# Cross-attention: the group maxima of the keys are copied between partition groups by ACT instead of being turned by TensorE

## The reference

```python
a = _layer_norm(audio_kv, ln_gamma, ln_beta)
Q = (hidden_states @ Wq.T) ...      # (B, 16, 512, 64)
K = (a @ Wk.T) ...
V = (a @ Wv.T) ...
scores = einsum('bhtd,bhsd->bhts', Q, K) * scale, masked keys at -inf
attn = softmax(scores, axis=-1)
out = einsum('bhts,bhsd->bhtd', attn, V) ... @ Wo.T
return hidden_states + tanh(gate) * out
```

## Time and profile before

| | |
|---|---|
| median of three runs | 2112.95 us |
| profiled execution, its own time | 2124.67 us |
| its span | 2122.9 us |
| granted clock of TensorE, mean | 0.992 |
| PE busy | 2024.5 us, 95% |
| DVE busy | 1709.6 us, 81% |
| POOL busy | 1510.0 us, 71% |
| ACT busy | 1127.6 us, 53% |
| share of PE in the chain that ended last | 71% |
| share of DVE in it | 18% |

### The profile page before, as it was taken

The page is one execution under the profiler, slowest core; times in us unless marked ns, Lnnn a source line. Parts: engine busy times, 40 slices in busy tenths (PEclk is TensorE's granted clock), DMA queues, the critical chain, the costliest instruction groups (busy, mean ns, idle before and its releaser), DMA issues.

```text
span 2122.9 us, 25985 instructions
## 1 busy us (share of the span) xinstructions
PE 2024.5 (95%) x8960; PEld 1589.0 (75%) x8960; DVE 1709.6 (81%) x2236; ACT 1127.6 (53%) x1578; POOL 1510.0 (71%) x830
## 2 busy tenths in 40 slices
PE   6999999999999999999999999999989999999996
PEld 4777777777777777777777777777767777777774
DVE  7788678887888878888788887888788888788785
ACT  4665744546544565445654556454554545644542
POOL 5999986567766687567866588666866668765664
PEclk9999999999999999999999999999999999999998
DMA  6566535444355334545236443355333553344331
GB/s 250 211 235 223 192 129 191 176 164 144 126 189 194 132 129 160 177 166 179 102 141 228 152 141 141 125 216 189 113 124 128 210 190 115 136 160 154 129 119 62
DMA packets 137219, 342.00 MB, mean 161 GB/s; under 512 B 56576, under 2 KB 57600, under 8 KB 136192
## 3 DMA queue, kind: packets, MB, share of 16 engines
q1 hardware_dynamic: 137088, 340.33, 45.5%
HBM read 288.89 MB, written 51.38 MB: 160 GB/s over the span
## 4 chain that ended last, share of the span: by engine, by line
PE 71%; DVE 18%; POOL 4%; issue 3%; ACT 3%; DMA 1%; SPq 1%; POOLq 0%; ACTq 0%; DVEq 0%
PE pj L435 13%; PE pj L439 13%; PE pj L437 12%; PE sc L387 5%; DVE prob L732 5%; PE sc L354 5%; PE sc L355 5%; PE sc L391 4%; PE sc L388 4%; PE pv L379 3%; PE pv L380 3%; DVE m_b L726 3%; DVE xy L777 2%; DVE mq L707 2%; PE pv L365 1%
## 5 line engine op out<-in xcount | busy, mean ns | idle before, releaser
L933 POOL TENSOR_TENSOR p_lo<-prob,p_hi 128x1024 fp32r<-128x1024 f32 x256 | 615.8, 2416 | 199.6 <-ACT p_hi L551 199.6
L707 DVE TRANSPOSE_TENSOR_REDUCE mq<-sc 128x32 f32<-128x1024 f32 x256 | 304.7, 1227 | 160.9 <-PE sc L355 160.7
L439 PE MATMUL pj<-a_hi,w_lo 128*128 128x512 f32 x1024 | 407.0, 397 | 0.0
L437 PE MATMUL pj<-a_lo,w_hi 128*128 128x512 f32 x1024 | 405.9, 396 | 0.0
L435 PE MATMUL pj<-a_hi,w_hi 128*128 128x512 f32 x1024 | 400.8, 391 | 3.6 <-POOL a_lo L967 1.4
L777 DVE SCALAR_TENSOR_TENSOR xy<-sc,tg_b,xy 128x1024 f32<-128x1024 f32 x256 | 321.1, 1272 | 42.9 <-PE sc L391 36.6
L570 ACT COPY o_tmp<-pv 64x512 f32<-64x512 f32 x128 | 74.3, 581 | 524.7 <-PE pv L380 524.6
L937 POOL TENSOR_TENSOR prob<-prob 128x1024 f32<-128x1024 f32 x128 | 308.2, 2408 | 0.0
L732 DVE TENSOR_TENSOR prob<-sc,m_b 128x1024 f32<-128x1024 f32 x256 | 301.5, 1219 | 4.4
L944 POOL TENSOR_TENSOR r_b<-o,r_b 128x512 f32<-128x512 f32 x64 | 83.3, 1302 | 311.5 <-DVE r_b L749 311.5
L546 ACT ACTIVATE prob<-prob 128x1024 f32<-128x1024 f32 x256 | 271.6, 1061 | 9.2 <-DVE prob L732 4.6
(11 more groups left out here) (88 smaller groups left out, 3854.2 us busy)
## 6 DMA issues: line engine op xcount, KB each, us to landing
w_hi<-kept_hi SPq DMA_DIRECT2D x225, 512.0 KB, 3.7
w_lo<-kept_lo SPq DMA_DIRECT2D x225, 512.0 KB, 4.6
cx<-in_ctx SPq DMA_DIRECT2D x32, 512.0 KB, 7.1
xy<-in_xT SPq DMA_DIRECT2D x32, 512.0 KB, 6.5
kept_hi<-w_hi SPq DMA_DIRECT2D x32, 512.0 KB, 5.6
kept_lo<-w_lo SPq DMA_DIRECT2D x32, 512.0 KB, 6.3
out_y<-xy SPq DMA_DIRECT2D x7, 2048.0 KB, 9.8
w_raw<-in_wq SPq DMA_DIRECT2D x8, 512.0 KB, 5.2
```

Source lines behind the costliest of these rows:

```text
L437: pe.matmul(dst[:, 0], w_hi[:, w, cols], s_lo[:, i], start=False, stop=False)
L439: mm = pe.matmul(dst[:, 0], w_lo[:, w, cols], s_hi[:, i], start=False, stop=i == KT - 1)
L707: dve.tensor_reduce(out=mq[:, 2 * i:2 * i + 2], in_=sc[:, 2 * i:2 * i + 2].rearrange("p s (b j) -> p s b j", j=32), op=ALU.max, axis=mybir ...
L933: pool.tensor_tensor(p_lo[:, 2 * i:2 * i + 2], prob[:, h, 2 * i:2 * i + 2], f32(p_hi[:, 2 * i:2 * i + 2]), ALU.subtract).then_inc(pl_done, 1)
```

## The change

The two PE transposes of a half go, with one DVE reduction and the tiles `m_cols`, `m_rows` and `m_two`. In their place ACT copies the 32x16 pieces of `m_own` (the new name of the 128x16 maxima) from the four partition groups side by side into partitions 0 to 31 of `m_four` (`gather_maxima`, four copies), DVE reduces them into the first group of `m_all` (`key_maxima`, 32x16), and ACT copies that group to the three others (`hand_out_maxima`, three copies). `spread_maxima` reads `m_all` in SBUF where it read a bank of `pv`. Each of the seven copies is an instruction of its own.

The names of two DVE functions change place: `group_maxima` is now the 128x16 reduction and `key_maxima` the one that combines the groups.

`FILL` is now (5, 4, 5, 2, 20) for half 0 and (5, 4, 7, 2, 18) for half 1: with the transposes gone there is one piece less, and the first number that follows the second `values` is 5 or 7, where it was 2 behind a 5 and a 2.

On ACT the new copies stand, in half 0, behind `o_high` (and behind the first `x_high` of "prepare", and the four `a_high` of "switch") and ahead of `split_w`, the other three `x_high` and `o_move`; in half 1 behind the second `q_high` and ahead of `split_w`, four `x_high` and `o_move`.

```diff
-FILL = ((5, 5, 2, 2, 2, 20), (5, 5, 2, 2, 2, 20))
+FILL = ((5, 4, 5, 2, 20), (5, 4, 7, 2, 18))
...
-            def maxima_turned(k, h):
-                pe.wait_ge(mc_done, k * 2 + h + 1)
-                ge(pe, oadd_done, k * 2 + h - 1)
-                pe.transpose(pv[h][:, 0, 0:P], m_cols[:], ident[:]).then_inc(mf_done, 1)
-
-            def maxima_back(k, h):
-                pe.wait_ge(mr_done, k * 2 + h + 1)
-                pe.transpose(pv[h][:, 0, P:2 * P], m_rows[:].rearrange("p c i -> p (c i)"), ident[:]).then_inc(mt_done, 1)
...
+            def gather_maxima(k, h):
+                act.wait_ge(mo_done, k * 2 + h + 1)
+                for c in range(4):
+                    act.copy(m_four[:, c], m_own[groups[c]]).then_inc(mf_done, 1)
+
+            def hand_out_maxima(k, h):
+                act.wait_ge(ma_done, k * 2 + h + 1)
+                for g in range(1, 4):
+                    act.copy(m_all[groups[g]], m_all[groups[0]]).then_inc(mv_done, 1)
...
-                split_w(b, WV, j + 1)
                 if kind == "prepare":
-                    for i in range(KT // 2):
-                        x_high(k, b, i, (b + 1) % 2)
+                    x_high(k, b, 0, (b + 1) % 2)
                 if kind == "switch":
                     for i in range(KT // 2, KT):
                         a_high(k, b, i)
+                gather_maxima(k, 0)
+                hand_out_maxima(k, 0)
+                split_w(b, WV, j + 1)
+                if kind == "prepare":
+                    for i in range(1, KT // 2):
+                        x_high(k, b, i, (b + 1) % 2)
                 if begun:
                     o_move(k - 1, 1)
...
                     q_high(k, 1)
+                gather_maxima(k, 1)
+                hand_out_maxima(k, 1)
+                if not last:
                     split_w(b, WQ, j + 2)
...
             def key_maxima(k, h):
+                dve.wait_ge(mf_done, k * 8 + 4 * h + 4)
+                dve.tensor_reduce(out=m_all[groups[0]], in_=m_four[:].rearrange("p c b -> p b c"), op=ALU.max,
+                                  axis=mybir.AxisListType.X).then_inc(ma_done, 1)
...
             def spread_maxima(k, h):
-                dve.wait_ge(mt_done, k * 2 + h + 1)
+                dve.wait_ge(mv_done, k * 6 + 3 * h + 3)
                 dve.transpose(m_b[:].rearrange("p (b i) -> p b i", i=32),
-                              pv[h][:, 0, P:P + 16].rearrange("p (b o) -> p b o", o=1).to_broadcast((P, 16, 32))
-                              ).then_inc(mb_done, 1)
+                              m_all[:].rearrange("p (b o) -> p b o", o=1).to_broadcast((P, 16, 32))).then_inc(mb_done, 1)
```

More of the change, by code:

```diff
@@ L72, in xattn_kernel @@
         m_b, r_b = sb("m_b", [P, T]), sb("r_b", [P, T])
-        mq, m_cols, m_rows = sb("mq", [P, TB, 16]), sb("m_cols", [P, P]), sb("m_rows", [P, 4, 32])
-        m_two = sb("m_two", [P, 64])
+        mq, m_own = sb("mq", [P, TB, 16]), sb("m_own", [P, 16])
+        m_four, m_all = sb("m_four", [32, 4, 16]), sb("m_all", [P, 16])
         rq, r_four = sb("rq", [P, 2, 16]), sb("r_four", [P, 4, 16])
@@ L103, in xattn_kernel @@
         init_done, row_done, mask_done, mrow_done = sem("init_done"), sem("row_done"), sem("mask_done"), sem("mrow_done")
-        mq_done, mc_done, mg_done, mr_done, mb_done, sub_done = (
-            sem("mq_done"), sem("mc_done"), sem("mg_done"), sem("mr_done"), sem("mb_done"), sem("sub_done"))
+        mq_done, mo_done, mf_done, ma_done, mv_done, mb_done, sub_done = (
+            sem("mq_done"), sem("mo_done"), sem("mf_done"), sem("ma_done"), sem("mv_done"), sem("mb_done"), sem("sub_done"))
         rq_done, rsum_done, rinv_done, rb_done = sem("rq_done"), sem("rsum_done"), sem("rinv_done"), sem("rb_done")
@@ L138, in xattn_kernel @@
         halves = (slice(0, HD), slice(HD, P))
+        groups = [slice(32 * g, 32 * (g + 1)) for g in range(4)]
         def splits(b, kind, pair):
@@ L373, in values @@
             def values(k, h, i):
-                if i == 0 and h == 0:
-                    pe.wait_ge(vl_done, k + 1)
+                if i == 0:
+                    ge(pe, oadd_done, k * 2 + h - 1)
+                    if h == 0:
+                        pe.wait_ge(vl_done, k + 1)
                 pe.wait_ge(pl_done, k * 4 + 2 * h + i + 1)
@@ L470, in body @@
                         pe.wait_ge(mrow_done, 2)
-                        pe.wait_ge(init_done, 7)
+                        pe.wait_ge(init_done, 5)
                     if j == 0 and h == 0 and not (isinstance(k, int) and k == 0):
@@ L479, in body @@
                         values(*before, 0)
-                    maxima_turned(k, h)
                     take(stream, f[1])
-                    maxima_back(k, h)
-                    take(stream, f[2])
                     if started:
@@ L487, in body @@
                         turn_v(k)
-                    take(stream, f[3])
+                    take(stream, f[2])
                     out_step(k, h, 0, kind)
@@ L492, in body @@
                         turn_ctx(k, b, 4 * h + 1)
-                    take(stream, f[4] if kind != "prepare" else f[4] + 4)
+                    take(stream, f[3] if kind != "prepare" else f[3] + 4)
                     out_step(k, h, 1, kind)
@@ L497, in body @@
                         turn_ctx(k, b, 4 * h + 3)
-                    take(stream, f[5] if kind != "prepare" else f[5] - 4)
+                    take(stream, f[4] if kind != "prepare" else f[4] - 4)
             def drain():
@@ L688, in _ @@
             act.copy(w_hi[:, WV], w_raw[:, 0]).then_inc(whi_done, 1)
-            act.wait_ge(init_done, 7)
+            act.wait_ge(init_done, 5)
             mask_rows(-1, -1)
@@ L709, in block_maxima, with group_maxima @@
                     apply_transpose=True).then_inc(mq_done, 1)
+            def group_maxima(k, h):
+                dve.wait_ge(mq_done, k * 4 + 2 * h + 2)
+                dve.tensor_reduce(out=m_own[:], in_=mq[:].rearrange("p s b -> p b s"), op=ALU.max,
+                                  axis=mybir.AxisListType.X).then_inc(mo_done, 1)
             def key_maxima(k, h):
[L712 to L722 removed]
+                dve.wait_ge(mf_done, k * 8 + 4 * h + 4)
+                dve.tensor_reduce(out=m_all[groups[0]], in_=m_four[:].rearrange("p c b -> p b c"), op=ALU.max,
+                                  axis=mybir.AxisListType.X).then_inc(ma_done, 1)
             def spread_maxima(k, h):
[L725 removed]
+                dve.wait_ge(mv_done, k * 6 + 3 * h + 3)
                 dve.transpose(m_b[:].rearrange("p (b i) -> p b i", i=32),
[L727 to L728 removed]
+                              m_all[:].rearrange("p (b o) -> p b o", o=1).to_broadcast((P, 16, 32))).then_inc(mb_done, 1)
             def subtract(k, h, i):
@@ L833, in body @@
                 block_maxima(k, 0, 1)
+                group_maxima(k, 0)
                 key_maxima(k, 0)
-                group_maxima(k, 0)
                 spread_maxima(k, 0)
@@ L856, in body @@
                 block_maxima(k, 1, 1)
-                key_maxima(k, 1)
+                group_maxima(k, 1)
                 if not last:
                     q_low(k, 1)
-                group_maxima(k, 1)
+                key_maxima(k, 1)
                 spread_maxima(k, 1)
@@ L883, in drain @@
                     accumulate(k, 2, n, n, n % 2, (B - 1) % 2)
-            dve.memset(m_cols[:], 0.0).then_inc(init_done, 1)
-            dve.memset(m_rows[:], 0.0).then_inc(init_done, 1)
             dve.memset(masked[:], MASKED).then_inc(init_done, 1)
```

12 lines of the change are left out of this document (1 added, 11 removed).

## The result

The changed kernel takes 2125.60 us, the median of four runs (2122.12 to 2127.49), against 2112.68 us for the kernel before beside it (2112.22 to 2113.77). The ratio is 1.0059, with a 95% interval of 1.0041 to 1.0076: 0.6% slower. A second set of five runs (experiment 1) gave 1.0075 (1.0063 to 1.0088). The time lies in the predicted range (2072 to 2132) and in the forecast's own range (2102 to 2128). "The same" was the forecast, though, and slower is what came.

The account below looks back on a forecast made before the run. PE's work plus its waits for DVE was taken as the bound; -5 us for 57 bodies and +6 us for seven "prepare" bodies gave +1 us, a forecast of 2114 us, range 2072 to 2132.

Parts of the forecast that it names:

- the forecast's own range: Whole kernel: 2102 to 2128 us, from copies at 0.215 to 0.245 us, engine changes at 0.03 to 0.05, and batch 0's bound.
- The same: Whole kernel: time within 0.2% (4.2 us) of the kernel before; chance 0.22.
- The price of a copy and the hold: ACT's copies: 0.204 us each, no overlap when source or target moves, so 0.23 us from start to start.
- Rivals A and B: ACT's copies: A, all overlap, 2048 us, chance 0.10; B, only a moved target ends the overlap, 2077 us, chance 0.14.
- Rival C: ACT's copies: few partitions cost 0.33 us from start to start, as L578 shows; 2198 us; chance with milder forms 0.09.
- The chain, L382 and plain halves: Plain halves: chain 2.24 us, output projection starting at 7.79 us, halves of 15.64 and 15.19 us, a body 0.09 us shorter.
- Prepare: "Prepare" bodies, ACT's queue: +0.5 us in half 0, +0.35 in half 1; seven bodies +6 us.
- Switch: "Switch" bodies: counted among the 57 bodies that are not "prepare", each 0.09 us shorter.
- Batch 0: Batch 0, ACT's queue: `split_w` later by 2 to 4 us, priced at nothing, with a bound of +4 us.
- Rival D: ACT's queue replaces the transposes as the wait; "prepare" and batch 0 lose twice the price, +10 us: 2123 us; chance 0.07.
- The sum: Whole kernel: -5 us for 57 bodies and +6 us for seven "prepare" bodies, together +1 us.
- The base of the sum: +1 us put the profiled execution at 2125.7 for 2124.67; the median, 11.7 us below that execution, gave 2114 us.

Follow-up runs that it names:

- experiment 1: The changed kernel once more, no edit, five executions: 2127.41 us, ratio 1.0075 to the kernel before.
- experiments 6 and 7: Changed kernel, one run each: all four gather copies reading one partition group, 2099.89 us; all three hand-out copies writing one group, 2098.14 us.
- experiment 8: The kernel before with two fills of half 1 moved from behind the output projection to ahead of it: 2090.98 us, ratio 0.9888.
- experiment 5: The kernel before once more, no edit, one execution for a second profile: 2114.75 us, span 2113.0 us.
- experiment 9: The changed kernel with the WQ split in half 1 of body 5 of batch 0 put back ahead of the copies: 2121.87 us, ratio 1.0044.
- experiment 4: The changed kernel with `split_w` (WV, batch 0 only) put ahead of the copies in half 0: 2141.28 us, ratio 1.0139.

## Why the prediction was right, and where it was not

**The price of a copy and the hold: right.** 203 and 202 ns for the 204 worked out from ACT's two casts, and 0.23 us from start to start, as forecast. Rivals A and B were wrong on this alone: no overlap was to be seen in the gather or in the hand-out, and experiments 6 and 7 brought it back (0.11 us) by keeping the source or the target still. Rival C's 0.33 us was as wrong; L578 was no guide for a plain copy.

**The chain, L382 and plain halves: right.** 2.20 us for 2.24; 7.74 and 7.71 us into the half for 7.79; halves of 15.65 and 15.17 us for 15.64 and 15.19. PE's tail behind L382 is 7.91 and 7.46 us for 7.85 and 7.40, 0.06 us longer than the earlier trace rows gave it, which makes up for L382's starting as much earlier. The two halves of a batch in which DVE comes late lost 0.40 and 0.49 us, as the plain half 1 does (0.43): also as written.

**"Prepare": the sum right, its split not.** +0.81 us for +0.85. Half 1 took +0.08 for +0.35, half 0 +0.73 for +0.5. In half 0 the exponential of body 30 starts 8.26 us into the half for 7.49 before, and PE waits 1.7 us for 1.2 at the second part of the output projection. In half 1 everything upstream came as forecast. Timeline of body 30 in experiment 1 (the half starts at 1029.43):

```profile
1035.13 2.18 ACT L598 CAST x_hi<-xy 128x512 fp32r<-128x512 f32 x4
1037.22 0.58 ACT L572 COPY o_tmp<-pv 64x512 f32<-64x512 f32 x1
1037.70 1.06 ACT L548 ACTIVATE prob<-prob 128x1024 f32<-128x1024 f32 x1
...
1043.70 0.42 PEld L449 LDWEIGHTS sc<-ident,cx 128*128 128x128 f32 x4 [1.66 <-ACT cx L602]
```

The exponential starts at 8.27 us of the half for the 8.5 forecast (7.71 before), and PE waits at the transposed context as I expected. The delay is 0.56 us and not 0.8, and 0.56 - 0.45 = +0.11 is near the +0.08 of the half. Most of the missing 0.24 us is overlap: `o_move` starts at 1037.22, 0.09 us before the last `x_high` has ended, and the exponential 0.48 us after it, where I took the 0.61 of the earlier trace rows.

**"Switch": taken for a plain body, wrong.** +0.31 us for -0.09. Half 1 is not shortened: it takes 15.70 us before and after, because the next body's scores wait for the row of the mask at the tail of ACT's queue. Experiment 1, the end of a "switch" body:

```profile
1077.67 1.46 ACT L580 ACTIVATE kt<-mask_u,masked 1x512 fp32r<-1x512 uint8 x2
...
1079.19 0.19 PEld L356 LDWEIGHTS sc<-qt,kt 128*128 128x128 f32 x1 [0.52 <-ACT kt L580]
```

The same wait was 0.16 us before. Fewer fills behind L382 only lengthen it: in experiment 8, on the kernel before, it is 0.63 us, and the half is again 15.70 us long. Seven such bodies are some 3 us that the sum did not have.

**Batch 0: the mis-sized term.** I wrote that `split_w` "is later by 2 to 4 us; the loads that hang on it have a body's time, so I price it at nothing, with a bound of +4 us". It measured +6.1 and +9.0 us, beyond its bound too. What I looked at was the loads behind the splits. The splits' second half is POOL's `w_lo`, and POOL is busy for 238 of the 256 us of that batch (experiment 5), so it has little room to catch up an idle stretch that a late split makes. Experiment 9 puts the late splits of body 5 at 0.7 us of POOL's time and the DVE instruction of 2.44 us, where it comes, at 2.3. Bodies 6 and 7 hold 5.6 of the 6.1 us, and 6.7 of the 9.0, 2.8 to 3.0 of them in the three halves behind half 0 of body 6; what delays those is not shown. Experiments 4 and 9 show that the place of a split in ACT's queue counts either way: early in half 0 the copies stand behind a load, late in half 1 POOL stands behind the copies. Rival D, which made ACT's queue the wait that replaces the transposes and doubled "prepare" and batch 0 to reach 2123 us, came nearest to the time. Its batch 0 was the right half of it, its "prepare" was not.

A second part of batch 0's loss was in no term and in no rival: the granted clock. PE's waits in the batch add up to 16.2 us in experiment 5, and to 24.8 and 28.6 us in the two profiles of the changed kernel. The clock granted in it falls short of full speed by 0.1 us in experiment 5 (length times the share not granted), and by 4.8 and 1.7 us in the other two. In half 0 of body 6 it is 0.93 in both where it was 1.00. How the 6.1 and 9.0 us divide between waits and clock isn't shown, since a slow stretch costs nothing while PE waits anyway.

**The sum.** For one of the batches 1 to 6 my terms give 6 x -0.09 = -0.5 us for the plain bodies, +0.85 for "prepare" and -0.09 for "switch", together +0.2. Measured: -0.7, +0.8 and +0.3, together +0.4. Of the 7.3 us between the traces, then, 3.3 lie in the six steady batches, where the terms gave 1.3, and 6.1 in batch 0, where they gave nothing; batch 7 and the stretch ahead of batch 0 give some 2 back. The forecast within 0.2% of no change was thus missed by batch 0, while the steady batches came out nearly as added up.

**The base of the sum.** I took the difference from the profiled execution of before, with its stall, and carried it over to the median. The stall is in neither half that I read, so the difference was not hurt by it.

**What stays open.** The traces differ by 7.3 and 10.0 us, the medians of the runs by 12.9 and 15.4. In both sets of the changed kernel the profiled execution was the fastest one. In experiment 1 the clock fits this: it was 0.993 in the profiled execution and 0.990 to 0.991 in the other four, which is 4 to 6 us of full speed. In the first set it doesn't: the profiled execution has 0.991 at 2122.12 us and another 0.993 at 2124.42. Batch 0 was seen at 255.6 to 264.8 us in traces of kernels with the copies (280.8 in experiment 4) and at 252.5 to 255.8 in those without. Its length varies with the clock, whose shortfall in this batch was 1.7 to 7.5 us in these kernels (14.3 in experiment 4) and at most 1.7 in those without the copies, and with the DVE instruction of 2.44 us, which five of the ten traces with the copies have. No execution of a median time was traced, so where its last 5 us lie isn't shown.

## What to carry to other kernels

When a change frees slots on one engine and lengthens a chain elsewhere, place the first instruction that depends on the chain anew before judging the change: two fills in either half were worth 42 us here, and the change as it stood cost 13. Give the kernel before the same chance: with its own two fills moved it was only 8 us behind. Price what is pushed back in a queue in the stage that is busiest, which was batch 0 and not the steady state, and by the engine that it feeds there too, not by its own deadline alone. Look at the granted clock of such a stage as well as at its waits. Small copies in a row on ACT cost their full length each when source or target moves between partition groups.
